# New slots for side work in a fused LayerNorm, recurrent-memory and gated-FFN kernel, and a LayerNorm written as product and sum

## The reference, cut to what matters

```python
xn = _layernorm(x, axis=-1)
# recurrence: q, k, v = xn Wq', xn Wk', xn Wv'
def step(M, qkv):
    q_t, k_t, v_t = qkv
    r_t = q_t @ M.T
    outer = v_t.T @ k_t / b
    M_new = DECAY * M + outer
    return (M_new, r_t)
s = (retrieved @ Wo') * sigmoid(gate)
# feed-forward on xn, F = 2048
h = (xn - mu) * jax.lax.rsqrt(var + EPS) * ln_gamma + ln_beta
y = jax.nn.silu(hf @ w1 + fc1_bias)      # w1 = (fc1_q - 128) * scales, 512 x 2048
z = y @ w2 + fc2_bias                    # w2 = (fc2_q - 128) * scales, 2048 x 512
g = _silu(xn + 0.5 * z)
x = x + s * g
```

## Time and profile before

| | |
|---|---|
| median of 3 runs | 1263.76 us (1263.10 to 1264.02) |
| the profiled execution | 1263.97 us, of which the span from first to last instruction is 1262.1 us |
| granted PE clock | 0.985 of full speed over the span |
| busy | PE 95%, DVE 90%, ACT 73%, POOL 62% of the span |

### The profile page before, as it was taken

The page is one execution under the profiler, slowest core; times in us unless marked ns, Lnnn a source line. Parts: engine busy times, 40 slices in busy tenths (PEclk is TensorE's granted clock), DMA queues, the critical chain, the costliest instruction groups (busy, mean ns, idle before and its releaser), DMA issues.

```text
span 1262.1 us, 18951 instructions
## 1 busy us (share of the span) xinstructions
PE 1196.1 (95%) x6028; PEld 618.3 (49%) x6028; DVE 1135.1 (90%) x1965; ACT 916.6 (73%) x1590; POOL 777.7 (62%) x766
## 2 busy tenths in 40 slices
PE   2799999999999999999999999999999999999994
PEld 1344555545555554555555455555545545555551
DVE  7799899999998999999898999999898999999887
ACT  6688677777767777776777777777786777778673
POOL 6067747749474783947569384765947477494732
PEclk9799999999999999999999999999999999999997
DMA  9511130402103030120302112040210304020011
GB/s 331 182 35 34 26 76 1 101 1 65 37 15 86 1 94 8 49 53 3 99 1 68 34 38 64 1 100 2 67 34 20 82 1 101 1 59 9 26 43 35
DMA packets 41620, 65.68 MB, mean 52 GB/s; under 512 B 11696, under 2 KB 11952, under 8 KB 41008
## 3 DMA queue, kind: packets, MB, share of 16 engines
q1 hardware_dynamic: 41232, 64.36, 19.1%
q10 hardware_dynamic: 288, 0.08, 0.0%
HBM read 47.59 MB, written 16.81 MB: 51 GB/s over the span
## 4 chain that ended last, share of the span: by engine, by line
PE 77%; DVE 10%; ACT 7%; issue 4%; POOL 1%; DMA 1%; SPq 0%; ACTq 0%; DVEq 0%
PE blk L492 29%; PE blk L510 27%; PE side L452 6%; PE side L477 4%; PE side L441 3%; DVE blk L772 3%; ACT blk L638 2%; PE side L428 2%; DVE g_lo L742 2%; DVE tops L810 1%; ACT z_rows L664 1%; DVE y_split L763 1%; DVE y_split L758 1%; PE side L470 1%; PE side L471 1%
## 5 line engine op out<-in xcount | busy, mean ns | idle before, releaser
L772 DVE TENSOR_TENSOR blk<-blk,ratio_rows 128x512 f32<-128x512 f32 x960 | 647.8, 690 | 109.8 <-PE blk L510 101.0
L638 ACT ACTIVATE blk<-blk,ratio 128x512 f32<-128x512 f32 x768 | 510.0, 665 | 258.6 <-PE blk L492 250.1
L492 PE MATMUL blk<-h_split,q_sb 128*128 128x512 f16 x2048 | 612.5, 381 | 11.7 <-ACT blk L638 5.0
L510 PE MATMUL blk<-w_sb,y_split 128*128 128x512 f16 x2048 | 610.4, 380 | 4.9 <-POOL w_sb L1085 1.9
L510 PEld LDWEIGHTS blk<-w_sb,y_split 128*128 128x128 f16 x2048 | 198.9, 98 | 254.2 <-issue 12.9
L492 PEld LDWEIGHTS blk<-h_split,q_sb 128*128 128x128 f16 x2048 | 193.5, 98 | 229.9 <-issue 36.8
L645 ACT ACTIVATE y_full<-blk,par,last 128x512 f32<-128x512 f32 x256 | 200.7, 784 | 54.7 <-PE blk L492 54.3
L763 DVE SCALAR_TENSOR_TENSOR y_split<-y_full,up,y_split 128x512 f16<-128x512 f32 x256 | 224.3, 876 | 0.0
L1076 POOL CAST h_split<-h_full 128x512 f16<-128x512 f32 x64 | 42.6, 665 | 252.8 <-ACT h_full L594 252.7
L758 DVE TENSOR_SCALAR y_split<-y_full,up 128x512 f16<-128x512 f32 x256 | 152.5, 596 | 0.0
L1064 POOL TENSOR_SCALAR g_rows<-xt,mv,gs 128x512 f32<-128x512 f32 x60 | 130.7, 2187 | 0.0
(11 more groups left out here) (155 smaller groups left out, 1133.0 us busy)
## 6 DMA issues: line engine op xcount, KB each, us to landing
xt<-in_x SPq DMA_DIRECT2D x64, 256.0 KB, 4.8
x_again<-in_x SPq DMA_DIRECT2D x256, 64.0 KB, 1.9
out<-z_rows SPq DMA_DIRECT2D x256, 64.0 KB, 1.7
w_sb<-in_q SPq DMA_DIRECT2D x4, 1024.0 KB, 13.8
ratio_rows<-ratio_dram SPq DMA_DIRECT2D x4, 1024.0 KB, 9.0
y_split<-in_q SPq DMA_DIRECT2D x1, 1024.0 KB, 10.3
h_split<-in_q SPq DMA_DIRECT2D x1, 1024.0 KB, 12.6
z_rows<-in_q SPq DMA_DIRECT2D x1, 1024.0 KB, 14.2
```

Source lines behind the costliest of these rows:

```text
L492: mm = pe.matmul(blk[J % 2][:], q1_sb[:, g, j // 4, w, j % 4 * P:(j % 4 + 1) * P], a[:, c % 2, g, :], start=(g == 0 and n == 0), stop=(g = ...
L510: mm = pe.matmul(blk2[:, i, :], y[:, J % Y_RING, rows], w2_sb[:, j, part, :], start=(j == 0 and n == 0), stop=(j == FB - 1 and n == len(te ...
L638: act.activation(blk[J % 2][:], blk[J % 2][:], ACT.Copy, scale=ratio1[:, at:at + 1]).then_inc(blk_scaled, 1)
L772: dve.tensor_tensor(blk2[:, i, :], blk2[:, i, :], ratio2_rows[:, j, :], ALU.mult).then_inc(blk2_scaled, 1)
```

## The change

Six entries of the table move, and the normalising of chunks 1 to 15 takes the form that chunk 0 had already.

- `TURN_AT`: the turns go from slots 52, 54, 56, 59 to 46, 50, 54, 58; what follows them (`g_hi`, `h_full`, `g_lo`, the fp16 split of h) follows at the same lags.
- `STATS_AT`, `MOMENTS_AT`: the next chunk's statistics go from slots 0 to 3 to slots 10, 14, 18, 22, the moments from 5 and 6 to 26 and 27; `ROWS_AT` goes from 7 to 28.
- `GATE_AT`, `ADD_AT`, `OUT_AT` and the last two of `PREPARE_AT` come four slots earlier.
- `NORMALISE_AT` comes two slots earlier. `(x - mean) * scale` becomes `x * scale + shift`; the shift is made by two more small POOL operations per chunk.

```diff
@@ -18,8 +18,7 @@
-ROW_STEPS = 10
-FIRST_SHIFT_STEPS = 2
+ROW_STEPS = 12
@@ -37,22 +36,22 @@
-TURN_AT = (52, 54, 56, 59)
+TURN_AT = (46, 50, 54, 58)
...
-GATE_AT = (16, 17, 21, 29)
-
-STATS_AT, MOMENTS_AT = (0, 1, 2, 3), (5, 6)
+GATE_AT = (12, 13, 17, 25)
+
+STATS_AT, MOMENTS_AT = (10, 14, 18, 22), (26, 27)
...
-NORMALISE_AT = (36, 38, 40, 42)
-PREPARE_AT, ROWS_AT, FIRST_ROWS_AT = (0, 3, 15, 18), 7, 28
+NORMALISE_AT = (34, 36, 38, 40)
+PREPARE_AT, ROWS_AT, FIRST_ROWS_AT = (0, 3, 11, 14), 28, 28
...
-ADD_AT, OUT_AT = (13, 14, 17, 20), (18, 22, 26, 30)
+ADD_AT, OUT_AT = (9, 10, 13, 16), (14, 18, 22, 26)
@@ -1012,9 +1011,11 @@
-            def first_normalise(i):
-
-                pool.tensor_scalar(g_rows[:, i, :], xt[:, i, :], gs[:, 0, i:i + 1], first_shift[:, i:i + 1],
+            def normalise(c, i):
+
+                if i == 0 and c > 0:
+                    pool.wait_ge(turn_done, 4 * c)
+                pool.tensor_scalar(g_rows[:, i, :], xt[:, i, :], gs[:, c % 2, i:i + 1], g_shift[:, c % 2, i:i + 1],
                                    ALU.mult, ALU.add).then_inc(g_done, 1)
@@ -1040,11 +1041,11 @@
+                step(pool.tensor_tensor(t[3], mean, gs[:, parity, :], ALU.mult))
+                step(pool.tensor_tensor(g_shift[:, parity, :], t[3], row_const[:, MINUS_ONE, :], ALU.mult))
                 if c == 0:
-                    step(pool.tensor_tensor(t[3], mean, gs[:, parity, :], ALU.mult))
-                    step(pool.tensor_tensor(first_shift[:], t[3], row_const[:, MINUS_ONE, :], ALU.mult))
                     for i in range(NT):
-                        first_normalise(i)
+                        normalise(0, i)
@@ -1056,13 +1057,6 @@
-            def normalise(c, i):
-                if i == 0:
-                    pool.wait_ge(rows_done, c + 1)
-                    pool.wait_ge(turn_done, 4 * c)
-                pool.tensor_scalar(g_rows[:, i, :], xt[:, i, :], mv[:, c % 2, i, 0:1],
-                                   gs[:, c % 2, i:i + 1], ALU.subtract, ALU.mult).then_inc(g_done, 1)
```

More of the change, by code:

```diff
@@ L242, in build @@
         gs = sb("gs", [P, 2, NT], F32)
-        first_shift = sb("first_shift", [P, NT], F32)
+        g_shift = sb("g_shift", [P, 2, NT], F32)
         v2 = sb("v2", [P, 4, NT], F32)
@@ L1025, in rows @@
                 t = [v2[:, n, :] for n in range(4)]
-                count = [ROW_STEPS * c + (FIRST_SHIFT_STEPS if c > 0 else 0)]
+                count = [ROW_STEPS * c]
                 def step(ins):
```

## The result

The changed kernel takes **1286.14 us** (median of 4 runs, 1285.55 to 1286.30), beside 1263.43 us for the kernel before (median of 4). The ratio is 1.0178 [1.0161, 1.0196]: slower by 22.7 us. The forecast was 1282 us. The profiled execution took 1285.55 us, of which the span is 1283.7 us, 21.6 us more than before.

What follows compares the result with a forecast made beforehand. PE (95% busy) came first, with DVE (90%) close behind and common to both stall clusters. The profiled 1263.97 us plus 9.6 for the turns and 8.4 for statistics and output gave 1282 us, range 1257 to 1303 for 8 in 10.

Steps and rivals of the forecast that it cites:

- The signs that it named: Profile after: turn waits at slots 50, 54; slots 18, 19, 63 free of ACT; holds at 24, 27, 64; chunk 75.9 us.
- Turns, slots 50 and 54: Turns four slots apart in a bank wait for `g_low`: 0.74 us at slot 50, 0.9 at slot 54.
- Turns, slot 64: `ffn2` of slot 64 waits for the `y_low` of slot 61, behind the last `g_low`: 0.4 us.
- The silu's stall of slot 63 goes: Slot 63's 0.32 us stall disappears, since ACT's two extra pieces per turn are now four slots apart.
- Chunk 0: Chunk 0, the last chunk's end and the start were taken as nothing, 2 us either way.
- Statistics and output, +8.4: Statistics in slots 10 to 22 and output four slots sooner: +0.60 us per chunk in chunks 1 to 14.
- 8.70 + 1.18 = 9.88: DVE's busy us from 587.40 to slot 21's `y_low` plus two statistics; `ffn2` of slot 24 starts 0.1 later.
- +0.70 at slot 27: The third statistic delays `remember` in a stretch without idle time, so the `wo` loads at 603.04 instead of 602.34.
- in the 8.70 already: The waits of DVE's `y` pieces for POOL were counted as already inside DVE's 8.70 us of busy time.
- inside this figure: The gain of freed slots 18 and 19 (0.31 and 0.23) lies within slot 27's +0.70, not to be had besides.
- Product and sum, 0: POOL's normalising takes 772 ns instead of 2187, saving 5.7 us per chunk, but nothing waits for it.
- Rival 3: DVE and POOL in worse step: one more full meeting (1.16) in slots 14 to 21, plus slot 61's; 1309 us, chance 0.17.

Runs made afterwards that it cites:

- the narrow run: The changed kernel with POOL's instructions for the output on 16 of 512 columns, leaving out the rest of the output: 1266.41 us.
- The spread version: The changed kernel with turns at 46, 53, 56, 59 and the output's work spread over the chunk: 1239.94 us, ratio 0.9812.

## Why the prediction was right, and where its steps were not

The sign and the size came out: +22.7 us against +18. That the sum came so near is partly luck. The turns cost some 19 us, chunk 0 included, where it had 9.6, and the rest of the change 2.8 where it had 8.4, so misses of 9.5 and 5.6 us in opposite directions left one of about 4. The signs that it named are there, with two exceptions. The `wo` of slot 27 does not wait for `remember`, and the 30 waits of turns for `g_low` are not "as before": the trace of before shows 15.

- **Turns, slots 50 and 54: right.** 0.74 and 0.87 measured, 0.74 and 0.9 said, and the stalls at 56 and 59 went as worked out.
- **Turns, slot 64: right in mechanism, too small.** 0.69 instead of 0.4. The prediction had the meeting with POOL's split of h and its full price, 0.85, and took the mean length of `y_low`. The meeting happened: 1.48 us against the mean of 0.88. The Trainium skill's page "SBUF — State Buffer" (section "SBUF: two separate sides") would have made it the full price, and the trace agrees with it here and in slots 12 to 24 of the narrow run, where no long POOL instruction stood beside and each `y_low` took 0.74 or 0.75. It does not agree everywhere: see the slow form of the normalising in the last section.
- **"The silu's stall of slot 63 goes": wrong.** It moved. Slot 62 has 0.30 now, since ACT's `h_full` of the turn of 58 stands in front of the rescaling of slot 61, which `ffn1` of slot 63 waits for. Together with slot 64 this makes +1.20 per chunk instead of +0.64, and in 14 chunks 16.8 us.
- **Chunk 0: too small.** Beyond one chunk's share of the turns (+0.64) it was taken as nothing, and it costs +2.3. Its turns of slots 50 and 54 are 3.23 and 2.81 us long. DVE, ACT and POOL still work on the weights there; no run shows that this is the cause.
- **Statistics and output, +8.4: wrong, it was +0.20 per chunk, 2.8 us.** `ffn2` of slot 24 came 0.47 later than before, counted from slot 1, instead of 0.1, and slot 27 then gave back 0.13 instead of adding 0.6. The step that failed is the addition of statistics to DVE's busy time ("8.70 + 1.18 = 9.88", and "with no idle time", +0.70 at slot 27). The 8.70 busy us held time in which DVE was blocked by POOL. The prediction knew this ("in the 8.70 already") and took that time as fixed. Blocked time is not work: when DVE comes later, it may meet more of it or less. In the run with the statistics alone slot 27 did not move, since the `y_high` of slot 23 met 0.59 less, and with the change's other parts the statistics even gained 2.4 us. Narrow POOL work took slot 24's 1.15 away with every statistic in place. What holds slot 24 is how long the `y` pieces before it are held by POOL's instructions, most of all when one is issued just after POOL's has begun. (The two moments, which the prediction put before slot 14, stand at 26 and 27, and slot 27 is free all the same.) That slots 18 and 19 would be freed was right; that this would be "inside this figure" was not, as slots 27 and 31 were freed as well, and it was slot 24 that took it back.
- **Product and sum, 0: right for the arithmetic, not for its place.** Alone, with its two small operations in front of the output's work, it costs 10 us, and with them behind it nothing. In the change they stand behind it too, with the row scales at 28; it was not undone there by itself.
- **Rival 3** (a worse step between DVE and POOL) had the mechanism right at both places: one more full meeting, which came at slot 12 and not in its slots 14 to 21, and the one of slot 61. Its 1.16 is also what the six `y` pieces of slots 12 to 21 show, 2.40 less 1.19 = 1.21. It was priced on top of the statistics' +8.4, which did not come; with it alone, the freed slots 18, 19, 27 and 31 nearly paid for slot 24.

Left open: whether there is an alignment in which the output's work, at full width and packed as here, does not reach slot 24. The spread version shows only that pauses help. Nor was it separated how much of slot 24's 1.15 is the meeting of slot 12 and how much those of slots 16 and 20. The statistics have a part in the first of these: with them alone in the kernel before, the `y_high` of slot 12 took 1.46 as well, and with the output moved but no statistics there it took 0.71, while slots 16 and 20 took 1.66 and 1.55.

## What to carry to other kernels

A buffer that is handed back in the very slot before it is wanted stalls its next user. Keep the two users of a bank a few slots further apart than the lag of its last reader: here turns six slots apart cost nothing, five slots 0.34 and four 0.74 or 0.87, and a `wo` five slots behind a turn nothing to 0.17. On an engine that another can block, busy time is not demand: look for the single operations that are much longer than the shortest of their form, see what began just before them, and ask whether the engine has idle time behind them before the result is wanted. Where it has none, spreading the other engine's work can be worth more than taking work off your own. The parts of such a change do not add (48 us alone, 22.7 together), so test each both alone and taken out of the whole, and move a stalling operation only after asking what is queued behind its new place.

## What the runs showed of the hardware

- A `y_high` (tensor_scalar, fp32 to fp16, 128x512) takes 0.48 us undisturbed and 1.47 to 1.55 when issued up to 0.08 us after a POOL tensor_tensor of 1.26 us. It ends about 0.3 us after POOL's. A `y_low` takes 0.74 and up to 1.81, and ends about 0.55 after POOL's. When the two begin together it can also be POOL that is held. In the kernel before, chunk 7, a `y_high` issued 0.03 us after a POOL instruction takes its 0.47, and the POOL instruction 1.06 instead of the 0.77 that others of its form take. In every such row the POOL instruction is a tensor_scalar. A `y_high` that is issued as close behind a tensor_tensor is held for all of it, as the one at 220.68 in the run without turns and statistics. What decides between the two is not shown.

```profile
569.48 0.47 DVE L758 TENSOR_SCALAR y_split<-y_full,up 128x512 f16<-128x512 f32 x1
```

```profile
569.45 1.06 POOL L1106 TENSOR_SCALAR xz<-x_again,row_z 128x512 f32<-128x512 f32 x1
```

- POOL's normalising takes 2187 ns as subtract and multiply, and 816 as multiply and add, on the same 128x512. I had not expected that this slow form blocks DVE only for part of its length. In the kernel before, DVE between 612 and 615, and POOL's three pieces around it:

```profile
612.52 0.47 DVE L758 TENSOR_SCALAR y_split<-y_full,up 128x512 f16<-128x512 f32 x1
...
614.10 1.21 DVE L763 SCALAR_TENSOR_TENSOR y_split<-y_full,up,y_split 128x512 f16<-128x512 f32 x1
```

```profile
609.44 6.64 POOL L1064 TENSOR_SCALAR g_rows<-xt,mv,gs 128x512 f32<-128x512 f32 x3
```

  The second of the three by itself; the third begins where it ends, at 614.02:

```profile
611.95 2.07 POOL L1064 TENSOR_SCALAR g_rows<-xt,mv,gs 128x512 f32<-128x512 f32 x1
```

  So the `y_high` at 612.52 was issued 0.57 us into its POOL instruction and was not held, while the `y_low` at 614.10 was issued 0.08 into the next and took 1.21. It ended 0.78 before POOL's instruction did. In the run with the statistics alone a `y_high` comes late in one, 1.53 in, and is held to 0.28 after its end (DVE, then POOL):

```profile
243.49 0.83 DVE L758 TENSOR_SCALAR y_split<-y_full,up 128x512 f16<-128x512 f32 x1
```

```profile
241.96 2.07 POOL L1064 TENSOR_SCALAR g_rows<-xt,mv,gs 128x512 f32<-128x512 f32 x1
```

  These rows fit a hold at the beginning and at the end of the instruction with none in its middle. No experiment was made on it, so this is a reading and its reason is open.
- Half a microsecond of small POOL operations, moved from ahead of the output's work to behind it, was worth 10 us of 1264, since the pattern repeats in each of 14 chunks.
